# Attention of a two-layer block on one core: from rounds over batch and key head to four segments in one pipeline, with projections made transposed and placed by DMA

## What is computed

```python
mod = (silu(c) @ wmod).reshape(2, 6, 1, -1)        # sa, ca, ga, sb, cb, gb
h = layernorm(x) * (1 + ca) + sa
x = x + ga * attn(h)       # window of 128 keys, causal, rope, bias, a sink per head
h = layernorm(x) * (1 + cb) + sb
u = h + attention(rmsnorm(h, ln1_w), wq, wk, wv, wo)      # causal over 512 keys
x = x + gb * (u + moe(rmsnorm(u, ln2_w), gate_w, w1, w2, w3))   # 8 experts, the best 2
```

## Time and profile before

| | |
|---|---|
| median of 3 runs | 1265.08 us (1264.76 to 1265.37) |
| the profiled execution, its own time | 1265.95 us |
| its span, first to last instruction | 1264.1 us |
| busy: PE, PEld | 1079.2 us (85%), 982.7 us (78%) |
| busy: DVE, ACT, POOL | 1011.4 us (80%), 777.1 us (61%), 327.9 us (26%) |
| mean granted clock of PE | 0.937 |
| chain that ended last, by engine | PE 64%, DVE 16%, issue 8%, ACT 6% |

### The profile page before, as it was taken

How to read it: one execution, slowest core, us unless ns; L and a number is a source line. 1 busy time by engine, 2 the same in 40 slices (tenths; PEclk the granted TensorE clock), 3 DMA queues, 4 the chain that set the end, 5 groups by cost and what they waited for, 6 DMA issues and landing times.

```text
span 1264.1 us, 27532 instructions
## 1 busy us (share of the span) xinstructions
PE 1079.2 (85%) x7484; PEld 982.7 (78%) x7484; DVE 1011.4 (80%) x3184; ACT 777.1 (61%) x2299; POOL 327.9 (26%) x544
## 2 busy tenths in 40 slices
PE   4699999999999992899999999999997349989892
PEld 1478888878888882689999989999996338888892
DVE  5599998989899998688888888888886716665655
ACT  2266666666566663688787878777776315554541
POOL 4455554545545448000000101000000220000013
PEclk9599999999999997699999999999999559999997
DMA  8600000000000000000000000010000345554413
GB/s 308 205 23 2 23 22 1 21 1 21 8 15 21 1 1 22 22 1 23 2 21 0 21 0 21 5 66 0 1 1 12 105 151 149 148 158 138 134 44 102
DMA packets 37400, 63.78 MB, mean 50 GB/s; under 512 B 3419, under 2 KB 23707, under 8 KB 37147
## 3 DMA queue, kind: packets, MB, share of 16 engines
q1 hardware_dynamic: 28604, 51.69, 13.1%
q10 hardware_dynamic: 7168, 6.88, 1.7%
q0 software_dynamic: 1536, 4.20, 1.1%
HBM read 45.92 MB, written 16.84 MB: 50 GB/s over the span
## 4 chain that ended last, share of the span: by engine, by line
PE 64%; DVE 16%; issue 8%; ACT 6%; DMA 2%; POOL 1%; ACTq 1%; DVEq 1%; SPq 1%; POOLq 0%
PE psO L621 14%; PE psS L593 9%; PE psX L604 8%; PE psP L640 8%; PE psY L675 5%; PE psS L792 4%; PE psX L792 3%; PE psT L651 3%; DVE pbuf L1185 3%; PE psT L660 2%; PE psO L813 2%; PE psP L813 2%; DVE pbuf L1201 2%; DVE bufB L1207 2%; DVE bufA L1243 1%
## 5 line engine op out<-in xcount | busy, mean ns | idle before, releaser
L880 ACT ACTIVATE pbuf<-pbuf,nmax 128x256 f32<-128x256 f32 (+3 forms) x512 | 266.9, 522 | 172.9 <-DVE nmax L1185 162.3
L621 PE MATMUL psO<-bufB 128*128 128x256 f32 x1632 | 257.4, 294 | 11.9 <-DVE bufB L1211 11.2
L593 PE MATMUL psS<-bufA 128*128 128x256 f32 (+3 forms) x1024 | 216.5, 317 | 19.9 <-DVE bufA L1243 16.9
L621 PEld LDWEIGHTS psO<-bufB 128*128 128x128 f32 x1632 | 213.5, 190 | 23.1 <-issue 12.7
L1207 DVE TENSOR_TENSOR bufB<-psX,bufB 128x512 fp32r<-128x512 f32 x272 | 186.7, 686 | 29.0 <-ACT bufB L853 27.0
L853 ACT ACTIVATE bufB<-psX 128x512 fp32r<-128x512 f32 x272 | 160.4, 590 | 59.5 <-PE psO L621 48.8
L593 PEld LDWEIGHTS psS<-bufA 128*128 128x128 f32 x1024 | 149.4, 194 | 37.5 <-DVE nmax L1185 26.0
L604 PE MATMUL psX<-idn,pbuf 128*128 128x128 f32 x1088 | 167.2, 276 | 2.7 <-DVE bufB L1207 2.2
L640 PE MATMUL psP<-wbufs,hTh 128*128 (+1 forms) x512 | 163.0, 360 | 1.6 <-DVE bufB L1236 1.6
L1201 DVE TENSOR_SCALAR pbuf<-pbuf,rden 128x256 f32<-128x256 f32 (+3 forms) x384 | 154.3, 457 | 4.5
L604 PEld LDWEIGHTS psX<-idn,pbuf 128*128 128x128 f32 x1088 | 124.5, 141 | 18.0 <-issue 8.4
(11 more groups left out here) (196 smaller groups left out, 2304.0 us busy)
## 6 DMA issues: line engine op xcount, KB each, us to landing
mrawV<-in_w_moe SPq DMA_DIRECT2D x32, 384.0 KB, 3.2
mrawB<-in_w_moe SPq DMA_DIRECT2D x32, 384.0 KB, 3.3
xg<-uN SPq DMA_DIRECT2D x1, 5248.0 KB, 23.8
yg<-uN SPq DMA_DIRECT2D x1, 5248.0 KB, 37.9
xin<-xg ACTq DMA_DIRECT2D x10, 384.0 KB, 3.8
wraw<-in_w_attn SPq DMA_DIRECT2D x8, 384.0 KB, 3.2
wraw<-in_w_ffn SPq DMA_DIRECT2D x8, 384.0 KB, 3.0
yg<-modb ACTq DMA_DIRECT2D x9, 256.0 KB, 2.2
```

Source lines behind the costliest of these rows:

```text
L593: last = mm(psS[j % 2][:, 0:n], qT[:, s % NT, j * P:(j + 1) * P], kT[:, c, k0:k0 + n], start=(c == 0), stop=(c == 1))
L621: last = mm(psO[:, 0:2 * P], lhsT, pairs(pT)[:, r], start=(k == 0 and n == 0), stop=(k == L.ntiles(s) - 1 and n == 5))
L880: nc.scalar.activation(pj, pj, ACT.Exp, bias=nmax[:, s % 4, j:j + 1], scale=-1.0, accum_out=sums[:, s % 4, j:j + 1]).then_inc(a_exp, 1)
```

## The change

**One pipeline.** The 128 units now run as four segments of 32: layer A batch 0, layer A batch 1, layer B batch 0, layer B batch 1. Inside a segment key heads are the outer loop and the four query tiles the inner one (`u % TB`). Sixteen units (four key heads) are a quad. Nothing is a hardware loop any more: PE's, DVE's, ACT's, POOL's and SP's lists are written out for all 128 units. The norms, features and residuals of a batch stand between the steps of the other batch's segment (`between`, and `turned` for the feature transposes).

**Transposed projections.** q and k are projected with the weights as the stationary operand and 512 rows of a batch as columns, so they come out transposed, and the twelve turning transposes, `write_qT` and `write_kT` go. A schedule by the unit's place m in its quad (`ahead`) gives at most one **item** per unit: ten q or k items (six products of 512 columns), four v items (six of 256 columns, a seventh for the bias), and two units without. In the windowed segments DVE takes a q or k item by two operations of 128x512 (`rope`), and POOL makes six operations of 128x512 per pair of items. In the causal segments ACT and DVE split the item. The result `st` (1 MB) is stored to DRAM by SP and read back by four (k in causal: two) transfers in the layout that the scores need (`place_q`, `place_k`), into two alternating slots.

**y in PSUM.** psT is gone, and two banks psY hold the four output tiles of a segment over all eight key heads; `add_y` goes, and DVE reads each tile once a segment (`take_y`).

**Division on the output.** The multiplication of the probabilities by the reciprocal goes. Instead POOL spreads the four reciprocals over 256 columns (`spread`), PE transposes them into the projection's bank psP (`turn_scale`), ACT copies them out (`scale_of`, to rS), DVE multiplies the output with them (`scale_out`, to oS), and ACT and POOL split oS (`out_hi`, `out_low`).

The start loads the rope tables by token and turns them, brings in the q and k bias as per-partition columns with 16 small transfers from ACT, and makes the items of the first key heads before unit 0. The zeroing of xg and yg becomes 16 transfers that ACT issues, one after every second step of the first segment.

The core of the diff:

```diff
+def ahead(u):
+    quad, m = divmod(u, QUAD)
+    if m in (5, 8, 11, 14):
+        return ("v", quad + 1, m // 3 - 1) if quad + 1 < NQUAD else None
+    if m in (6, 7):
+        return ("k", quad + 1, m - 6) if quad + 1 < NQUAD else None
+    for first, part in ((0, 2), (3, 3), (9, 4), (12, 5)):
+        if m in (first, first + 1):
+            g = 4 * quad + part
+            return ("q", g, m - first) if g < NG else None
...
 # PE
+            def begin_item(item, u=None):
+                wait(pe, v_pj, ITEM[item] - 1)
+                if u is not None and u >= 2:
+                    pe.wait_ge(a_rx, min(u - 1, NU))
...
+                last = mm(psP[:, :], w[:, g % 2, k, i * P:(i + 1) * P], a[:, k, b * SEQ:(b + 1) * SEQ], ...)
...
+            def turn_scale(u):
+                pe.wait_ge(g_rx, u + 1)
+                pe.wait_ge(v_pj, BANKED[min(u + 1, NU - 1)])
+                wait(pe, a_rx, u)
+                for i in range(2):
+                    last = turn(psP[:, i * P:(i + 1) * P], rdenx[:, i * P:(i + 1) * P], idn[:, :])
+                last.then_inc(s_rx, 1)
...
 # ACT
+            def scale_of(u):
+                act.wait_ge(s_rx, u + 1)
+                wait(act, v_os, u - 1)
+                copy(rS[:, u % 2, :], psP[:, 0:2 * P]).then_inc(a_rx, 1)
+            def out_hi(u):
+                act.wait_ge(v_os, u + 1)
+                wait(act, s_Y, u - 1)
+                copy(oh[:, u % 2, :], oS[:, u % 2, :]).then_inc(a_oh, 1)
...
 # DVE
-                    for j in range(L.by_vector):
-                        pj = probs[:, s % 4, j, 0:n]
-                        last = V.tensor_scalar(pj, pj, rden[:, s % 4, j:j + 1], None, ALU.mult)
...
+            def scale_out(u):
+                dve.wait_ge(s_PV, KT[u + 1])
+                wait(dve, g_ol, u - 1)
+                dve.wait_ge(a_rx, u + 1)
+                V.tensor_tensor(oS[:, u % 2, :], psO[:, 0:2 * P], rS[:, u % 2, :], ALU.mult).then_inc(v_os, 1)
...
 # the order of a windowed step, ACT
+                exp_head(u, 0)
+                if u >= 3:
+                    out_hi(u - 3)
+                if nk > 0:
+                    scale_of(u - 2)
+                if nk > 1:
+                    probs_hi(u - 2, 1)
+                exp_head(u, 1)
...
 # the order of a windowed step, DVE
+                if u >= 1:
+                    denominator(u - 1)
+                mask_max(u, 0)
+                mask_max(u, 1)
+                if nk > 0:
+                    probs_lo(u - 2, 0)
+                if u >= 3:
+                    scale_out(u - 3)
+                if item:
+                    take(item)
+                mask_max(u, 2)
+                if nk > 1:
+                    probs_lo(u - 2, 1)
+                mask_max(u, 3)
```

More of the change, by code:

```diff
@@ L35 @@
 HD = 64
+HALF = HD // 2
 NKV, QM = 8, 4
@@ L93, in exists, with windowed @@
-def exists(g, s):
-    return not isinstance(g, int) or 0 <= NT * g + s < NT * NKV
-def wait(eng, sem, value):
-    if not isinstance(value, int) or value > 0:
-        eng.wait_ge(sem, value)
-def rounds(eng, step):
-    for s in range(-2, NT):
-        step(0, s)
-    with eng.Fori(1, NKV - 1) as g:
-        for s in range(NT):
-            step(g, s)
-    for s in range(NT + 5):
-        step(NKV - 1, s)
+SEGU = NKV * TB
+NU = 4 * SEGU
+QUAD = 4 * TB
+NQUAD = NU // QUAD
+NG = NU // TB
+def windowed(u):
+    return u < 2 * SEGU
@@ new lines, in turned, with prologue_items, by_scalar @@
+def turned(u):
+    seg, r = divmod(u, SEGU)
+    if r not in (14, 15):
+        return ()
+    return tuple(TB * (seg + 1) + 2 * (r - 14) + i for i in range(2))
+def prologue_items():
+    yield from (("f", t, 0) for t in range(TB))
+    yield from (("q", 0, i) for i in range(2))
+    yield from (("k", 0, i) for i in range(2))
+    yield from (("v", 0, t) for t in range(TB))
+    yield from (("q", 1, i) for i in range(2))
+def by_scalar(item):
+    kind, index, _ = item
+    if kind == "q":
+        return index >= NG // 2
+    if kind == "k":
+        return index >= NQUAD // 2
+    return True
@@ new lines, with count_items @@
+ITEM, HIGH, PAIR, OUT = {}, {}, {}, []
+def count_items():
+    every = list(prologue_items())
+    for u in range(NU):
+        if ahead(u):
+            every.append(ahead(u))
+        every += [("f", n, 0) for n in turned(u)]
+    high = 0
+    for p, item in enumerate(every):
+        ITEM[item] = p + 1
+        high += by_scalar(item)
+        HIGH[item] = high
+        if item[0] in "qk" and item[2] == 1:
+            PAIR[item[:2]] = len(PAIR)
+            OUT.append((OUT[-1] if OUT else 0) + (0 if item[:2] == ("k", 0) else 16))
@@ L533, in _ @@
+            split_wo(0)
+            rope_high(("q", 1))
+            rope_low(("q", 1))
+            split_wq(2)
+            for u in range(NU + 4):
+                step(u)
             pool.wait_ge(v_slot, 1)
-            pool.wait_ge(st_zero, 16)
+            pool.wait_ge(st_zero, 16 * 15)
             for t in range(NT):
@@ new lines, in take, with mask_max @@
+            def take(item):
+                if by_scalar(item):
+                    low(item)
+                else:
+                    rope(item[:2], item[2])
+            def mask_max(u, j):
+                h = QM * u + j
+                n = keys(u) * P
+                dve.wait_ge(s_S, h + 1)
+                if j == 0 and u >= TB:
+                    dve.wait_ge(s_X, KT[u - TB + 1])
+                apart(dve)
+                V.tensor_tensor_reduce(probs(u, j), psS[j % 2][:, 0:n], mcau[:, SEQ - n:], -SCALE, 3e38,
+                                       ALU.add, ALU.min, nmax[:, u % 4, j:j + 1]).then_inc(v_max, 1)
@@ new lines, in step_causal @@
+            def step_causal(u):
+                now = u < NU
+                item = ahead(u) if now else None
+                nk = keys(u - 2) if u - 2 < NU else 0
+                if now:
+                    mask_max(u, 0)
+                if u - 1 < NU:
+                    denominator(u - 1)
+                if now:
+                    mask_max(u, 1)
+                if nk > 0:
+                    probs_lo(u - 2, 0)
+                if nk > 1:
+                    probs_lo(u - 2, 1)
+                if u - 3 < NU:
+                    scale_out(u - 3)
+                if item:
+                    take(item)
+                if now:
+                    mask_max(u, 2)
+                if nk > 2:
+                    probs_lo(u - 2, 2)
+                if now:
+                    mask_max(u, 3)
+                if nk > 3:
+                    probs_lo(u - 2, 3)
+                between(u)
+                if now:
+                    for n in turned(u):
+                        low(("f", n, 0))
@@ new lines, in _ @@
+            for r in range(2):
+                dve.wait_ge(a_k0, r + 1)
+                last = V.tensor_tensor(st0[:, 1, r, :], tmp0[:, 2 * r, :], st0[:, 0, r, :], ALU.subtract)
+            last.then_inc(v_k0, 1)
+            for t in range(TB):
+                low(("v", 0, t))
+            for n in range(2, 3 * BATCH):
+                modulation_rows(n)
+            rope(("q", 1), 0)
+            rope(("q", 1), 1)
+            dve.wait_ge(v_mod, 6)
+            link(V.tensor_scalar(CB, CB, 1.0, None, ALU.add))
```

1680 lines of the change are left out of this document (949 added, 731 removed).

## The result

The changed kernel takes **1405.2 us** (median of 4 runs, 1400.46 to 1415.38) beside 1265.0 of the kernel before: 1.112 times, 95% interval 1.109 to 1.116. The forecast was 1255 with a range up to 1300. The profiled execution took 1400.63 us, with a span of 1398.7 beside 1264.1 before. The four runs lie 15 us apart, and the longer ones went with a lower mean granted clock (1400.5 us at 0.911, 1415.4 at 0.893); why was not tried.

The account below looks back on a forecast made before the run. It took PE and DVE as full in the windowed half, PE alone in the causal. Start +18, windowed +13, causal -36, end -5 sum to -10: 1255 us forecast, the case's own range 1228 to 1282, the 8-in-10 range ending at 1300.

Parts of the forecast that it names:

- What bounds after the change: Windowed half: DVE near 60% busy, idle until PE's item, which waits for ACT's copy to rS.
- this chain: Windowed step: one closed loop through DVE, ACT, PE and POOL, 7.9 us in the longest step, above both engines' work.
- Together 113.4/16 = 7.1 us, and 64 units take 454.: Windowed half: sixteen steps of the four-engine loop sum to 113.4 us, giving 7.1 us per unit.
- Norm and modulation ... 27 us: Windowed half: ACT-issued transfers, table loads with roots, norm and modulation, turned features, squares and gate rows add 27 us.
- the 4 in the causal half: Causal half: ACT and DVE work between the steps costs 4 us.
- so the chain is open and PE sets the pace.: Causal half: scale_of before the second exponential opens the loop; units go from 6.9 to 6.5 us, -36 us.
- the fourth rival: Causal half keeps 6.9 us per unit because waits for rS replace those for kT, time 1281; chance 0.08.
- The pace of 6.45: Causal half: the pace per unit before rounding to 6.5 us, used to take 416 us.
- The start: Before unit 0: features, items and modulation rows put the first mask at 70 to 71 us against 53.2, +18 us.
- The half clock: Rival: PE falls to half clock inside windowed steps, 1.0 us per unit, 65 us, time 1320; chance 0.08.
- The transfers: Rival: storing and placing q and k by DMA doesn't keep up, up to 60 us, time 1280 to 1315; chance 0.09.
- The end: After the last mask: four of eight last feature tiles are done earlier, -5 us.

Follow-up runs that it names:

- e1: Changed kernel with ACT issuing the copy to rS ahead of the copy to oh in windowed steps: 1334.2 us against 1405.2.
- e3: Changed kernel with turned reciprocals through psO instead of psP, items no longer waiting for the copy to rS, scale_of moved on ACT: 1309.9 us.
- e4: Changed kernel without the division (no spread, turn_scale, scale_of): windowed half 417.9 us against 537.1, causal 441.6 against 469.0; total time not compared.
- e14b: Changed kernel with POOL's windowed rope cut to 4 columns plus eight unread PE products per windowed step: windowed half 511.9 us against 537.1.
- e5: Changed kernel with one turned feature tile in each of four steps instead of two in each of two: 1389.9 us.
- e13b: Changed kernel with five square roots between first and last mask replaced by copies: first to last reciprocal 996.0 us against 1006.1.
- e15b: Changed kernel with DVE's modulations and norm multiplications between segments cut to 4 columns: first to last reciprocal 993.5 us against 1006.1.
- e10: Reciprocals through psO in windowed steps only, one feature tile a step (1286.2 us); then turn_scale, scale_of and spread first in causal steps: 1270.4 us.
- e9: Changed kernel with POOL splitting the third group's q weights ahead of its rope in the start: 1406.7 us.
- e11: Windowed-only psO reciprocals, one feature tile a step (1286.2 us); then start items alternating between psP and psO, all queues reordered: 1259.2 us.
- e2: Changed kernel with eight unread 256-column PE products in each windowed step's pause before the item: 1389.6 us.
- e8: Changed kernel with q and k stores and placements cut to 8 columns after the start: windowed half 537.1 us, causal 468.6, against 537.1 and 469.0.

## Why the prediction was wrong, point by point

**What bounds after the change: right.** DVE near 60% (55%), its idle time before L1448 ended by PE's L817, PE's before L817 ended by the copy to rS: all seen, and e1, e3 and e4 show that this chain is the cause in the windowed half.

**The failed step of the windowed half: "Together 113.4/16 = 7.1 us, and 64 units take 454."** Units outside a handover take 7.4 to 8.1 us. The chain was the right mechanism, and its first part was sized right: from the last exponential to the denominator 0.80 us for 0.78, from the first mask to the product with rS 1.30 for 1.30, from there to the copy to rS 0.77 for 0.76. What was mis-sized is the part behind it. From the copy to rS to the third mask the working has 0.36 + 1.55 + 1.25 = 3.16 us; at full clock it measures 3.57 (247.21 to 250.78 in the second step above), 0.4 more in ten of sixteen steps, by estimate 16 us over the half. At half clock the item takes 2.90 instead of 1.64 (225.01 to 227.91 in the first step), 17 us in all. The fillers and the shrunk rope together give 0.4 us per unit of the missing 0.6 to 0.7 back (e14b). The terms of the long step add up to 7.8, not to 7.9; that is 1 us in a quad and not what failed.

**"Norm and modulation ... 27 us" was the second failed term.** The four handovers, of eight units each, lie 17, 20, 21 and 12 us above neighbours of 7.7, 8.0, 7.0 and 7.2 per unit: 70 us (37 in the windowed half) against 27 and the 4 in the causal half, and those 27 held other items as well. In the two windowed ones DVE's denominator comes mostly 2.6 to 3.7 us behind the last exponential in place of 0.8. Without them, features, roots and norms gave back 15, some 10 and some 13 us (e5, e13b, e15b, each alone). The rest is not settled; the squares, POOL's gate rows and the sums of y weren't tried.

**The failed step of the causal half: "so the chain is open and PE sets the pace."** This is the largest error of sign, -36 forecast and +36 measured; handovers are 33 of the 72, for which the forecast had 4. The order of the list did open the loop, but PE still waited for the copy before its items: 24.6 us between 650 and 940 us, 37 units, 0.7 us each, and nearly every item starts 0.47 us after the copy to rS does. ACT in a causal step of the changed kernel:

```profile
855.51 0.62 ACT L1167 ACTIVATE pbuf<-pbuf,nmax 128x384 f32<-128x384 f32 x1 [0.76 <-DVE nmax L1481]
...
856.13 0.58 ACT L1136 ACTIVATE pTh<-psX 128x512 fp32r<-128x512 f32 x1
856.61 0.37 ACT L1136 ACTIVATE rS<-psP 128x256 f32<-128x256 f32 x1
```

and PE, whose turned reciprocals were there at 855.0:

```profile
857.08 0.35 PE L847 MATMUL psP<-wkvh,hTh 128*128 128x256 f32 x1 [0.62 <-issue]
```

The copy stands behind an exponential that waits for a mask and behind a copy of the probabilities. So the fourth rival (causal half without gain, 0.08, 6.9 us) was nearer: units outside a handover take 7.0 to 7.3 up to the last quad, which has fewer items and takes 6.1 to 6.5. That this wait is the price is shown in part: e10 moved it away for the first units and gave back 15 us. The pace of 6.45 without that wait was right at its best only: e4 has 6.45 and 6.50 and then 6.6 to 6.9, e10 6.48 and then 6.8 to 7.0.

**The start: mechanism right, +18 against +26.3, and what lay behind the first mask missed.** Each step named is in the trace, but not at its size: the first item starts at 34.1 us and not at 28, and the v items take 13 us (49.2 to 62.1) and not 9, 4.6 of them a single pause. Left out: two small DVE operations on the gate weights, 1.1 and 1.2 us, right before the first mask, and POOL's list, in which the weights of unit 0's item (83.2 us) stand behind a rope that began at 76.8, so that PE pauses 9.8 us. e9 shows that mending this order alone gains nothing in the end; e11 shows that the single bank and the order of all lists together cost 22 us.

**The rivals.** The half clock did come; lifting it to 0.95 gave 16 us in e2, against 65 priced for a clock at half in every item, and 17 of 39 had it wholly or in part. The transfers cost nothing in the two halves (e8). The rule of the Trainium skill on short runs ("DMA: Bandwidth & Descriptors", Specifications) put 4 us on the start; no run here separates them from the 26.

**The end: right**, -3.7 for -5.

**The range** failed because I took as independent what is one thing. Terms were taken at full clock and each in its own time, and a chain through four engines breaks both: it makes the pauses behind which the clock falls, and it puts work that used to be hidden on the path. Its errors add on one side. The bound of 521 for the windowed half had 7.6 us per unit and 35 us beside; it came to 7.8 and 37. The causal half had -10 as its upper bound and came to +36.

## What to carry to other kernels

Before a change takes work from two full engines, write down which semaphore each moved copy waits for and what stands in front of it in its own list: here one copy, one line too low in ACT's list, cost 71 us. If a single buffer (psP) is passed around by producer, copy and consumer, each new use of it puts the next one behind it; another bank, with the order that goes with it, gave 109 us in one half and took 13 in the other, so it is tried for each stage by itself. Where no engine was full (PE 73%, DVE 55%), the work of one engine said little about the pace; the loop through the lists did, and its terms are better taken from a stretch with pauses in it.

## What the runs showed of the hardware

- The clock can fall after a pause, in the work that follows. In this step of the changed kernel PE pauses 1.90 us; the item begins at full clock (products 0.23 to 0.24 apart behind the first), and from its last product on everything runs at half (256 columns 0.21 apart, where 0.11 to 0.12 is full clock at 857.5 us). The pause's length alone doesn't tell: behind pauses of 1.90 to 1.91 us the item at 304.0 us ran wholly at half, the one at 132.2 fell in its midst, and the one at 397.3 stayed at full clock. Eight unread products of 256 columns per step lifted the granted clock from 0.88 to 0.95 and made the kernel faster.

```profile
544.79 0.47 PE L830 MATMUL psP<-hTh,wkvh 128*128 128x512 f32 x1 [1.90 <-issue]
...
545.79 0.41 PE L830 MATMUL psP<-hTl,wkvh 128*128 128x512 f32 x1
546.03 0.60 PE L830 MATMUL psP<-hTh,wkvl 128*128 128x512 f32 x1
546.43 0.41 PE L933 MATMUL psY<-woh,oh 128*128 128x256 f32 x1
546.64 0.41 PE L933 MATMUL psY<-woh,ol 128*128 128x256 f32 x1
```

- DVE and POOL slow each other. The addition of the denominators, 128x4, took 0.228 us on average in the kernel before and 0.416 after (100 to 480 us), at worst 1.23. In the rows below it takes 1.22 while POOL works on 128x512. A product with two SBUF operands of 256 columns took 1.37 us in place of 0.48 during such an operation of POOL:

```profile
200.33 1.37 DVE L1419 SCALAR_TENSOR_TENSOR hb<-hb,rs,modb 128x256 f32<-128x256 f32 x1
201.62 1.22 DVE L1489 TENSOR_TENSOR den<-sums,esink 128x4 f32<-128x4 f32 x1
```

```profile
199.98 1.43 POOL L661 TENSOR_TENSOR tmp<-tmp 128x512 f32<-128x512 f32 x1
201.38 1.44 POOL L662 TENSOR_TENSOR tmp<-tmp 128x512 f32<-128x512 f32 x1
```

The Trainium skill's page "SBUF — State Buffer" (SBUF: two separate sides) says that a GpSimd instruction that reads SBUF and a VectorE instruction with two SBUF inputs need one shared pair of ports, and that whichever starts first holds it to its end. By that rule the addition starts late and lasts as long as POOL's operation; the trace agrees, and POOL's own 1.27 becomes 1.43.
